# A four-layer kernel on one core: the next layer's Wq, key and value weights folded and split within the closing stage, and both late blocks of the last closing stage loaded ahead of its stores

## The chip, the core and the metric

One core of a Trainium2 chip runs the whole program. The metric is the device time of one execution in microseconds (us); lower is better. The engines are PE (TensorE, matrix products), ACT (ScalarE), DVE (VectorE), POOL (GpSimd) and SP (SyncE), which here only issues DMAs, one after another.

## The reference, cut to what matters

```python
# x: 2 sequences of 1024 rows, 256 wide; cond: 2 x 64
x = x + mixture_of_experts(x, cond)                       # layer 0
for layer in (1, 2, 3):                                   # attention, 16 heads of 64
    xn = layernorm(x) * g_norm                            # g_in in layer 2
    q = xn @ Wq                                           # 256 x 1024
    k, v = split(xn @ Wkv)                                # one key and one value head for all 16
    k, v = concat(cond[0], k), concat(cond[1], v)         # the null key and value
    if layer != 2:
        q = l2norm(q) * q_scale; k = l2norm(k) * k_scale  # logits times 8
        bias = two_layer_network(distance)                # w0, b0, g0, w1, b1, g1, w2, b2
    else:
        q = q / 8; bias = fside                           # an input, 16 x 1024 x 1024
    out = causal_softmax(q @ k.T + bias) @ v
    x = x + layernorm(out @ Wout) * g_out
return x
```

## The kernel before

All matrix products run in a reduced fp32 format, so each operand is split into a high part (a rounding copy) and a low part (value minus high part), and a product is three matmuls (`three_products`, line 216). The rows of `x` stay in SBUF as 16 tiles of 128 rows; four tiles make a block.

Each of the layers 1 to 3 runs four stages. A stage is a `Phase`: each engine has its own list of instructions, linked by semaphores, and a barrier of all engines ends it. So a stage lasts as long as its slowest engine, and nothing of the next stage starts before.

- `prepare_layer` (the preparation). It waits for the layer's inputs (`loaded`). ACT multiplies Wq by the norm's gain (`fold`, line 926) and rounds it (`high_part`, line 932). The null key `k0n` is made (lines 735 to 750), multiplied into Wq (`null_products`, line 701), summed by head (line 771) into 16 further columns of the key and value weights `wx`; DVE scales the other columns by the gain (line 765) and splits `wx` (lines 774 and 776). The first block of `x` is standardised (line 854), turned by PE (line 692) and split (`first_high` on ACT, line 943, and `first_low` on DVE, line 862). DVE writes a mask penalty (line 755) and the null values (six copies, line 760). In layers 1 and 3 the bias network runs too: DVE and ACT alternate over two halves (variances end in line 801, the last silu and low part in lines 814 and 820), PE multiplies, and DVE writes the bias row from PE's last product (line 917). In layer 2 POOL makes the low part of Wq (`low_part`, line 711) and DVE does the products of line 701. In the layers 1 and 3 POOL does those products here and the low part of Wq at the start of `project` (line 1511). In layer 1 DVE also writes four rows of ones (line 870).
- `project`: queries, keys and values of four blocks; SP stores queries and loads first rows of bias.
- `attend`: scores, softmax and outputs; it writes the outputs to `o_dram` and already loads blocks 0 and 1 of them for the next stage.
- `close_layer` (the close). Per tile n of 16: ACT rounds the tile of outputs (`high`, line 1968), DVE makes its low part (`low`, line 2037), both two tiles ahead; PE does 24 matmuls and a product for the null weights; ACT copies the result (line 1974); DVE takes statistics (lines 2042 and 2044). Per block c of 4: variances on DVE (line 2049), root on ACT, and then DVE standardises four tiles (line 2057); for c below 3 POOL multiplies by `gain_out` and adds to `x` (lines 2108 and 2111), and for c = 3 DVE does both (lines 2063 and 2065), after it has waited for POOL's block 2. SP loads block 2 of the outputs once DVE has split block 0, then block 3 once block 1 is split, and then the next layer's inputs. In the last layer SP stores block c - 2 of `x` (`store`, line 1933) behind each of these two loads:

```python
                for c in range(2, NCH):
                    eng.wait_ge(s["o_lo"], CT * (c - 1))
                    load_outputs(eng, t, s[f"in{c % 2}"], c)
                    if out is not None:
                        store(eng, c - 2)
```

The trace names the tiles by where they lie: `bias` is also the space of `wq`, `wx`, `w1` and of the even output blocks, `o_in` that of the odd ones, `v` in the preparation that of the standardised first block.

## Time and profile before

| | |
|---|---|
| median of 3 runs | 2259.14 us (2256.57 to 2260.59) |
| the profiled execution, its own time | 2255.18 us |
| its span in the trace | 2253.4 us |
| mean granted PE clock | 0.943 of full speed |
| close of layer 1 | 855 to 919.7 us of the span |
| preparation of layer 2 | 920.7 to 937.7 |
| close of layer 2 | 1483 to 1547.6 |
| preparation of layer 3 | 1548.6 to 1594.1 |
| close of layer 3, with the last store | 2177.5 to 2253.4 |

A row of a timeline gives the start in us of the span, the duration (of all together where it ends in xN), engine, line, operation, output <- inputs with their shapes, and in brackets the idle time before it and what ended it. Durations of an instruction include the time in which it was issued but held.

### The profile page before, as it was taken

Reading aid. Unit: us, or ns where it says so; the run is one execution under the profiler, and the core shown is the slowest. Engines: PE = TensorE matmul, PEld = TensorE weight load, DVE = VectorE, ACT = ScalarE, POOL = GpSimd, SP = SyncE. Lnnn points to the kernel's source line nnn. Section 1 sums busy time; section 2 is a strip of 40 time slices with the busy share of each in tenths; the row PEclk is TensorE's granted clock in tenths of the full one; section 3 lists DMA queues with packets and bytes.
Section 4 is the critical chain, followed back from the end, with each engine's and each line's share of the span. In section 5 each row is a group of like instructions: output and inputs, shape, how many; then the busy total and the mean of one; then the engine's idle time right before and its main releaser. Section 6 shows DMA issues by size and latency. Waiting matters only on the chain. (4 is left out here: it accounts for less than half of the span.)

```text
span 2253.4 us, 46773 instructions
## 1 busy us (share of the span) xinstructions
PE 1968.3 (87%) x11698; PEld 1427.4 (63%) x11698; DVE 1687.6 (75%) x4098; ACT 1338.7 (59%) x2908; POOL 1077.4 (48%) x1301
## 2 busy tenths in 40 slices
PE   5998595999999998589999999985786999999987
PEld 4887463666666668466666666675554666666667
DVE  4777877877887785658777778758677888887855
ACT  2222565777776674247677667644665777766743
POOL 0443112666766662206666566623124666655622
PEclk8999697999999999799999999997897999999998
DMA  4630167333333343286777888840474333333422
GB/s 119 203 112 26 36 222 257 104 113 112 113 113 113 110 143 110 83 309 189 235 238 239 240 243 242 271 146 15 160 243 159 113 112 112 113 113 113 133 84 102
DMA packets 220535, 338.75 MB, mean 150 GB/s; under 512 B 25766, under 2 KB 102700, under 8 KB 220364
## 3 DMA queue, kind: packets, MB, share of 16 engines
q1 hardware_dynamic: 220364, 336.85, 47.2%
q8 instruction: 60, 0.98, 0.2%
q14 instruction: 111, 0.91, 0.1%
HBM read 250.62 MB, written 102.91 MB: 157 GB/s over the span
## 5 line engine op out<-in xcount | busy, mean ns | idle before, releaser
L1618 POOL TENSOR_SCALAR at_row<-at_row,at_inv 128x129 f32<-128x129 f32 (+7 forms) x384 | 715.5, 1863 | 356.8 <-DVE at_inv L1782 350.4
L1829 ACT ACTIVATE at_row<-at_row,at_nmax 128x129 f32<-128x129 f32 (+7 forms) x768 | 595.3, 775 | 235.2 <-DVE at_nmax L1801 233.7
L1801 DVE CUSTOM_DVE_ANT_0 at_row<-at_s,bias,at_row 128x128 f32<-128x128 f32 (+7 forms) x768 | 617.4, 810 | 70.6 <-PE at_s L1729 36.3
L1741 PE MATMUL at_t<-ident,at_row 128*128 128x128 f32 x3456 | 545.6, 281 | 40.1 <-ACT at_pt L1822 34.1
L1741 PEld LDWEIGHTS at_t<-ident,at_row 128*128 128x128 f32 x3456 | 393.2, 142 | 244.6 <-issue 164.5
L1728 PE MATMUL at_s<-k_hh,q_hl 128*128 128x512 f32 (+3 forms) x1152 | 463.1, 402 | 45.8 <-SPq L1686 21.6
L1757 PE MATMUL at_o<-at_pt,v 128*64 128x512 f32 (+3 forms) x2304 | 437.2, 501 | 5.6 <-ACT at_pt L1822 2.5
L1633 DVE COPY at_pt<-at_t 128x128 f32<-128x128 f32 (+3 forms) x576 | 277.9, 483 | 177.8 <-PE at_t L1741 174.1
L1729 PE MATMUL at_s<-k_lp,q_h 65*128 65x512 f32 (+3 forms) x1152 | 394.4, 354 | 0.0
L1822 ACT ACTIVATE at_pt<-at_t 128x512 f32<-128x512 f32 (+2 forms) x576 | 306.8, 533 | 133.9 <-PE at_t L1741 128.7
L1728 PEld LDWEIGHTS at_s<-k_hh,q_hl 128*128 128x128 f32 x1152 | 225.4, 196 | 79.3 <-DVE at_nmax L1801 31.5
L1757 PEld LDWEIGHTS at_o<-at_pt,v 128*64 128x64 f32 x2304 | 143.3, 136 | 179.2 <-issue 142.1
L1618 DVE TENSOR_SCALAR at_row<-at_row,at_inv 128x129 f32<-128x129 f32 (+7 forms) x384 | 253.0, 659 | 2.1 <-issue 0.9
L1729 PEld LDWEIGHTS at_s<-k_lp,q_h 65*128 65x128 f32 x1152 | 225.7, 196 | 17.7
L1829 ACT ACTIVATION_READ_ACCUMULATOR at_row<-at_row,at_nmax 128x1 f32 x768 | 144.0, 187 | 0.0
L1884 POOL COPY null_w<-at_row 128x2 f32 (+1 forms) x384 | 71.2, 186 | 132.8 <-DVE at_row L1618 70.4
L216 PE MATMUL cl_y<-wo_h,cl_oh 128*128 128x256 f32 x384 | 117.5, 306 | 15.5 <-DVE cl_ol L2037 15.5
L1872 POOL COPY at_row<-neg_null 128x2 f32 (+1 forms) x384 | 71.9, 188 | 104.2 <-PEq L145 80.5
L521 POOL TENSOR_TENSOR moe_hid_l<-moe_hid,moe_hid_h 128x512 fp32r<-128x512 f32 x40 | 51.7, 1293 | 142.2 <-ACT moe_hid_h L506 142.1
L216 PE MATMUL cl_y<-wo_l,cl_oh 128*128 128x256 f32 x384 | 112.0, 292 | 0.0
L216 PE MATMUL cl_y<-wo_h,cl_ol 128*128 128x256 f32 x384 | 111.8, 291 | 0.0
L1517 POOL TENSOR_TENSOR o_in<-pj_qn,o_in 128x512 fp32r<-128x512 f32 x26 | 36.1, 1392 | 123.2 <-ACT o_in L1275 123.2
(249 smaller groups left out, 2855.9 us busy)
## 6 DMA issues: line engine op xcount, KB each, us to landing
q_hl<-q_dram SPq DMA_DIRECT2D x192, 256.0 KB, 4.3
q_dram<-o_in SPq DMA_DIRECT2D x76, 512.0 KB, 3.7
bias<-bands_dram SPq DMA_DIRECT2D x64, 512.0 KB, 5.4
q_h<-q_dram SPq DMA_DIRECT2D x96, 256.0 KB, 5.0
o_dram<-o_sb SPq DMA_DIRECT2D x96, 256.0 KB, 4.6
bands_dram<-brow_dram SPq DMA_DIRECT2D x2, 8192.0 KB, 32.2
bias<-corners_dram SPq DMA_DIRECT2D x256, 64.0 KB, 4.3
bias<-in_fside SPq DMA_DIRECT2D x32, 448.0 KB, 4.8
```

The lines of the kernel that those rows point to most:

```text
L216: last = eng.matmul(out, left[a], right[b], start=start and n == 0, stop=stop and n == len(pairs) - 1)
L1618: return eng.tensor_scalar(cells, cells, inv[:, i:i + 1], None, ALU.mult)
L1633: copy(bass.AP(one.tensor, one.offset, [one.ap[0], [pitch, blocks], [1, P]]), t_ps[m % NTR][:, 0:blocks * P].rearrange("p (c i) -> p c i", ...
L1728: eng.matmul(out, q_hl[:, g % 2, side, at], t["k_hh"][:, b, c:c + n], start=True, stop=False)
L1729: last = eng.matmul(out, q_h1[0:DH + 1, g % 2, side, at], t["k_lp"][0:DH + 1, b, c:c + n], start=False, stop=True)
L1741: last = eng.transpose(t_ps[m % NTR][:, c * P:(c + 1) * P], row[:, u % RING, here:here + P], t["ident"][:])
L1757: last = eng.matmul(o_ps[side * DH:(side + 1) * DH, i0:BANK], t["v"][:, turn.half_of(GU * g) * NT + j, :], pt[g % 2][:, side, at + i0:at + ...
L1801: eng.tensor_tensor_reduce(out=row[:, u % RING, ZERO:ZERO + width], in0=s_ps[u % 2][:, 0:width], in1=bt[:, lo:lo + width], scale=-1.0, sca ...
L1822: return eng.activation(out, in_, ACT.Copy)
L1829: eng.activation(cells, cells, ACT.Exp, scale=-1.0, bias=nmax[:, i:i + 1], accum_out=rsum[:, i:i + 1]).then_inc(s["exp"], 1)
L1872: eng.tensor_copy(null_cell(u, 2), nulls(turn, "neg_null", u)).then_inc(s["null_in"], 1)
L1884: eng.tensor_copy(nulls(turn, "null_w", u), null_cell(u, 2)).then_inc(s["null_out"], 1)
```

## The change

The work on Wq and `wx` is cut into functions. For layer 1 they still run in the preparation. For the layers 2 and 3 (`coming`) they run in the close of the layer before: ACT folds and rounds Wq in tiles 11 to 14; DVE squares (or, for layer 2, scales) the null key and scales `wx` at tile 11, ends the null key of layer 3 at tile 13, sums the products at tiles 14 and 15, and splits `wx` before the last tile's statistics; POOL clears the spare columns of `wx` and does both products between its work on block 1 and block 2, and for layer 2 makes the low part of Wq after block 2. In layer 3's inputs the bias network's are loaded last. The rows of ones of layer 1 go from DVE to POOL. In the last close SP issues both loads first and all four stores behind them. To make room for `wq_h`, `wq_l`, `wx_h` and `wx_l` in the close, three tiles of the projection share space with tiles of the attention.

```diff
+WEIGHT_STEPS = ["norm_in", "norm", "folded", "k0n", "prod", "hi", "lo", "wx_zero"]
...
+def fold_gain(eng, t, s, k):
+    i = t["inputs"]
+    eng.activation(i["wq"][:, k, :], i["wq"][:, k, :], ACT.Copy, scale=i["gain"][:, k:k + 1]).then_inc(s["folded"], 1)
+def high_weights(eng, t, s, k):
+    eng.wait_ge(s["folded"], k + 1)
+    eng.activation(t["wq_h"][:, k, :], t["inputs"]["wq"][:, k, :], ACT.Copy).then_inc(s["hi"], 1)
+def low_weights_of(eng, t, s):
+    eng.wait_ge(s["hi"], KD)
+    for k in range(KD):
+        for n in range(2):
+            at = slice(n * BANK, (n + 1) * BANK)
+            eng.tensor_tensor(t["wq_l"][:, k, at], t["inputs"]["wq"][:, k, at], f32(t["wq_h"][:, k, at]), ALU.subtract
+                              ).then_inc(s["lo"], 1)
...
+def null_root(eng, s, space):
+    eng.wait_ge(s["norm_in"], 1)
+    eng.activation(space["ss"][:], space["ss"][:], ACT.Sqrt).then_inc(s["norm"], 1)
...
+def null_key(eng, own, t, s, space):
+    i, ss, k0n = t["inputs"], space["ss"], space["k0n"]
+    own.step(eng.scalar_tensor_tensor(t["kscale"][:], t["kscale"][:], 8.0, i["qcol"][:], ALU.mult, ALU.mult))
+    own.step(eng.scalar_tensor_tensor(i["kscale"][:], i["kscale"][:], 8.0, i["qs"][:], ALU.mult, ALU.mult))
+    eng.wait_ge(s["norm"], 1)
+    own.step(eng.tensor_scalar(ss[:], ss[:], 1e-12, None, ALU.max))
+    own.settle()
+    own.step(eng.reciprocal(ss[:], ss[:]))
+    own.settle()
+    eng.scalar_tensor_tensor(k0n[:], i["k0"][:], ss[:, 0:1], i["kscale"][:], ALU.mult, ALU.mult).then_inc(s["k0n"], 1)
...
+def null_products(eng, t, s, space):
+    eng.wait_ge(s["k0n"], 1)
+    for k in range(KD):
+        eng.wait_ge(s["folded"], k + 1)
+        eng.tensor_tensor(space["prod"][:, k, :].rearrange("p (h d) -> p h d", h=H),
+                          t["inputs"]["wq"][:, k, :].rearrange("p (h d) -> p h d", h=H),
+                          space["k0n"][:].unsqueeze(1).to_broadcast([P, H, DH]), ALU.mult).then_inc(s["prod"], 1)
...
+def key_gains(eng, own, t):
+    wx, gain = t["inputs"]["wx"], t["inputs"]["gain"]
+    for k in range(KD):
+        own.step(eng.tensor_scalar(wx[:, k, 0:NUL], wx[:, k, 0:NUL], gain[:, k:k + 1], None, ALU.mult))
+def null_sums(eng, own, t, s, space, k):
+    eng.wait_ge(s["prod"], k + 1)
+    own.step(eng.tensor_reduce(t["inputs"]["wx"][:, k, NUL:NUL + H], space["prod"][:, k, :].rearrange("p (h d) -> p h d", h=H),
+                               AX.X, ALU.add))
+def split_key_weights(eng, own, t, s):
+    wx = t["inputs"]["wx"]
+    eng.wait_ge(s["wx_zero"], 1)
+    own.settle()
+    own.step(eng.tensor_copy(t["wx_h"][:], wx))
+    own.settle()
+    own.step(eng.tensor_tensor(t["wx_l"][:], wx, f32(t["wx_h"][:]), ALU.subtract))
...
-                    null_products(eng)
-                    eng.wait_ge(s["prod"], 1)
-                else:
-                    low_part(eng)
-                    eng.wait_ge(s["lo"], 1)
+                if layer == 1:
+                    eng.memset(i["wx"][:, :, NUL + H:], 0.0).then_inc(s["wx_zero"], 1)
+                    eng.wait_ge(s["cleared"], 2)
+                    eng.wait_ge(s["wx_zero"], 1)
+                    for n in range(4):
+                        eng.memset(f32(t["q_h1"][DH:DH + 1, n // 2, n % 2, :]), 1.0).then_inc(s["ones"], 1)
+                        eng.wait_ge(s["ones"], n + 1)
+                    null_products(eng, t, s, space)
+                    eng.wait_ge(s["prod"], KD)
...
                 loaded(eng)
                 if not normed:
-                    null_square()
                     first_rows()
                     first_standardize()
-                    null_products(eng)
                     null_values()
                     first_low()
-                    null_columns()
-                    xo.settle()
+                    eng.wait_ge(s["v0_in"], 1)
+                    eng.wait_ge(s["x_lo"], KD)
                     return
-                null_square()
+                if layer == 1:
+                    null_square(eng, own, t, s, space, True)
...
-                null_key()
+                if layer == 1:
+                    null_key(eng, own, t, s, space)
...
                 for m in range(2):
                     silu(2 + m)
                     low_silu(2 + m)
-                    if m == 0:
-                        ones()
-                null_columns()
+                if layer == 1:
+                    for k in range(KD):
+                        null_sums(eng, own, t, s, space, k)
+                    split_key_weights(eng, own, t, s)
...
-        xb = sb("pj_xb", [P, CT, D])
+        xb = t["o_sb"][:].rearrange("p n i -> p (n i)").rearrange("p (n i) -> p n i", n=CT)
...
-            qn = sb("pj_qn", [P, NQN, BANK])
+            qn = t["wo_raw"].rearrange("p a n -> p (a n)").rearrange("p (n i) -> p n i", n=NQN)
...
+    WEIGHTS_AT = 11
+    coming = None if inputs is None else inputs[-1]
...
                 for c in range(2, NCH):
                     eng.wait_ge(s["o_lo"], CT * (c - 1))
                     load_outputs(eng, t, s[f"in{c % 2}"], c)
-                    if out is not None:
-                        store(eng, c - 2)
                 if inputs is not None:
                     load_inputs(eng, t, *inputs)
                 for n in range(2):
                     eng.wait_ge(s[f"in{n}"], 16)
                 if out is not None:
-                    for c in range(NCH - 2, NCH):
+                    for c in range(NCH):
                         store(eng, c)
                     eng.wait_ge(s["stored"], 16 * NCH)
...
+                    if coming and WEIGHTS_AT <= n < WEIGHTS_AT + 2 * KD:
+                        if n == WEIGHTS_AT:
+                            inputs_loaded(eng, t)
+                        if n < WEIGHTS_AT + KD:
+                            fold_gain(eng, t, s, n - WEIGHTS_AT)
+                        else:
+                            high_weights(eng, t, s, n - WEIGHTS_AT - KD)
+                    if coming == 3 and n == WEIGHTS_AT + 1:
+                        null_root(eng, s, space)
...
+                    if coming and n == WEIGHTS_AT:
+                        inputs_loaded(eng, t)
+                        null_square(eng, own, t, s, space, coming != 2)
+                        key_gains(eng, own, t)
+                    if coming == 3 and n == WEIGHTS_AT + 2:
+                        null_key(eng, own, t, s, space)
+                    if coming and n >= NTT - KD:
+                        null_sums(eng, own, t, s, space, n - NTT + KD)
+                if coming:
+                    split_key_weights(eng, own, t, s)
                 statistics(NTT - 1)
                 variances(NCH - 1)
                 close(NCH - 1)
...
                     eng.tensor_tensor(t["x"][:, at, :], t["x"][:, at, :], half, ALU.add).then_inc(s["added"], 1)
+                    if coming and c == NCH - 3:
+                        inputs_loaded(eng, t)
+                        eng.memset(t["inputs"]["wx"][:, :, NUL + H:], 0.0).then_inc(s["wx_zero"], 1)
+                        null_products(eng, t, s, space)
+                if coming == 2:
+                    low_weights_of(eng, t, s)
+                    eng.wait_ge(s["lo"], 2 * KD)
+                elif coming:
+                    eng.wait_ge(s["prod"], KD)
...
+        for layer in (0, 1, 2, 3):
+            w = inputs_of(layer)[0] if layer else None
             with tensors(nc) as (sbl, _):
                 for part in "hl":
                     t[f"wo_{part}"] = sbl(f"wo_{part}", [P, NPAIR, D], FR)
+                    t[f"xt_{'high' if part == 'h' else 'low'}"] = t[f"wo_{part}"][:].rearrange("p a n -> p (a n)").rearrange(
+                        "p (c k i) -> p c k i", c=2, k=KD)
                 t["o_sb"] = sbl("o_sb", [P, 2, BANK])
                 t["wo_raw"] = sbl("wo_raw", [P, NPAIR, D])[:]
-                attend(nc, t, w, bias)
-                close_layer(nc, t, out if layer == 3 else None, inputs_of(layer + 1) if layer < 3 else None)
+                if layer:
+                    t["gain_out"] = t["gains_out"][layer % 2]
+                    attend(nc, t, w, None if layer != 2 else a["fside"])
+                if layer == 3:
+                    close_layer(nc, t, out, None)
+                    break
+                with tensors(nc) as (sbq, _):
+                    for part in "hl":
+                        t[f"wq_{part}"] = sbq(f"wq_{part}", [P, KD, H * DH], FR)
+                        t[f"wx_{part}"] = sbq(f"wx_{part}", [P, KD, 2 * P], FR)
+                    if layer:
+                        close_layer(nc, t, None, inputs_of(layer + 1))
+                    normed = layer + 1 != 2
+                    if normed:
+                        t["bands_n"] += 16
+                    with tensors(nc) as (sbp, _):
+                        t["brow_sb"] = sbp("brow_sb", [H, BROW])
+                        prepare_layer(nc, t, layer + 1)
+                        project(nc, t, normed, None if normed else a["fside"])
```

## Rows read from the trace of the kernel before

**Rows 1.** The page's first part: busy us of each engine, share of the span, instructions.

```profile
PE 1968.3 (87%) x11698; PEld 1427.4 (63%) x11698; DVE 1687.6 (75%) x4098; ACT 1338.7 (59%) x2908; POOL 1077.4 (48%) x1301
```

**Rows 2.** The chain that ended last, two steps in the last close: start, us.

```profile
2214.99 0.39 SPq L1933
2215.43 8.90 DMA o_in<-o_dram
```

**Rows 3.** ACT's timeline, last close: start, us, operation, [idle before, releaser].

```profile
2224.35 1.06 ACT L1968 ACTIVATE cl_oh<-o_in 128x1024 fp32r<-128x1024 f32 x1 [6.78 <-DMA o_in<-o_dram]
```

**Rows 4.** DVE's timeline, preparation of layer 2.

```profile
924.64 2.35 DVE L701 TENSOR_TENSOR lw_prod<-bias,lw_k0n 128x1024 f32<-128x1024 f32 x2
...
928.58 3.82 DVE L760 COPY v0m<-in_v 64x8 f32<-64x8 f32 x6
...
934.22 2.33 DVE L771 TENSOR_REDUCE bias<-lw_prod 128x16 f32<-128x1024 f32 x2
...
937.05 0.69 DVE L776 TENSOR_TENSOR wx_l<-bias,wx_h 128x512 fp32r<-128x512 f32 x1
```

**Rows 5.** DVE's splits of output blocks, all closes: shortest, median, longest ns.

```profile
L2037 DVE TENSOR_TENSOR cl_ol<-bias,cl_oh x24: 1217/1222/2883, 856.9 to 2216.7; 128x1024 fp32r<-128x1024 f32 x24
```

**Rows 6.** POOL's split of Wq in layer 2's preparation: shortest, median, longest ns.

```profile
L711 POOL TENSOR_TENSOR wq_l<-bias,wq_h x4: 1257/1482/3139, 925.0 to 931.0; 128x512 fp32r<-128x512 f32 x4
```

**Rows 7.** DVE's timeline, preparation of layer 1.

```profile
245.71 1.22 DVE L787 TENSOR_TENSOR bias<-rb_mm,bias 128x1024 f32<-128x1024 f32 x1 [0.35 <-PE rb_mm L216]
...
261.33 2.11 DVE L870 MEMSET q_h<- 1x512 f32 x4 [0.16 <-issue]
```

**Rows 8.** ACT's timeline, preparation of layer 2.

```profile
926.78 1.08 ACT L943 ACTIVATE xt_high<-lw_xtr 128x512 fp32r<-128x512 f32 x2 [1.89 <-PE lw_xtr L692]
```

**Rows 9.** POOL's timeline, close of layer 1.

```profile
900.35 3.27 POOL L2111 TENSOR_TENSOR x<-x,cl_y 128x1024 f32<-128x1024 f32 x1
...
911.51 2.39 POOL L2111 TENSOR_TENSOR x<-x,cl_y 128x1024 f32<-128x1024 f32 x1
```

**Rows 10.** DVE's timeline, close of layer 1.

```profile
898.47 2.88 DVE L2037 TENSOR_TENSOR cl_ol<-o_in,cl_oh 128x1024 fp32r<-128x1024 f32 x1
...
914.43 0.43 DVE L2042 BATCH_NORM_STATS2 cl_stats<-cl_y 128x6 f32<-128x256 f32 x1 [0.75 <-ACT cl_y L1974]
...
918.44 1.23 DVE L2065 TENSOR_TENSOR x<-x,cl_y 128x1024 f32<-128x1024 f32 x1
```

**Rows 11.** DVE's timeline, preparation of layer 3.

```profile
1548.67 0.23 DVE L737 TENSOR_TENSOR lw_k0n<-in_k 128x64 f32<-128x64 f32 x1 [1.06 <-PEq L83]
...
1570.03 0.15 DVE L743 SCALAR_TENSOR_TENSOR kscale<-kscale,in_qcol 128x1 f32<-128x1 f32 x1
...
1570.62 0.28 DVE L750 SCALAR_TENSOR_TENSOR lw_k0n<-in_k,lw_ss,in_kscale 128x64 f32<-128x64 f32 x1
...
1573.92 1.88 DVE L801 TENSOR_SCALAR rb_rstd<-rb_mv 128x4 f32<-128x4 f32 x1
...
1580.34 0.64 DVE L760 COPY v0m<-in_v 64x8 f32<-64x8 f32 x6
...
1592.83 1.27 DVE L917 TENSOR_SCALAR brow_sb<-rb_mm,in_b 16x1024 f32<-16x1024 f32 x1
```

**Rows 12.** POOL's timeline, preparation of layer 3.

```profile
1571.08 4.70 POOL L701 TENSOR_TENSOR lw_prod<-bias,lw_k0n 128x1024 f32<-128x1024 f32 x2 [20.61 <-DVE lw_k0n L750]
```

**Rows 13.** PE's timeline, last product in the preparation of layer 3.

```profile
1591.70 0.63 PE L216 MATMUL rb_mm<-rb_uh,rb_w2l 128*128 128x512 f32 x1
```

**Rows 14.** DVE's timeline, close of layer 2.

```profile
1535.52 1.38 DVE L2057 TENSOR_SCALAR cl_y<-cl_y,cl_mv,cl_rstd 128x256 f32<-128x256 f32 x4
...
1546.38 1.22 DVE L2065 TENSOR_TENSOR x<-x,cl_y 128x1024 f32<-128x1024 f32 x1
```

**Rows 15.** Two stretches of layer 2's projection: busy us, then clock, DMA.

```profile
938.00:950.00 12.00, 10.91 (x40) 8.77 (x41) 4.83 (x16) 3.24 (x7) 0.00 (x0) 0.75 0.62 179
...
965.00:980.00 15.00, 14.32 (x69) 11.16 (x68) 9.98 (x25) 6.85 (x14) 0.00 (x0) 1.00 0.83 276
```

143 lines of the change are left out of this document (43 added, 100 removed).

## The prediction, made before the changed kernel ran

> **What bounds the kernel now.** I read the page's first part first: PE is busy for 87% of the span [rows 1]. That is an average; this change touches only stage ends, where PE rests. So I read next the chain that ended last. It ends in the last close, and there a load of outputs waits its turn: SP stands in front of a store that needs POOL's block 0, issues the store at 2214.99, then the load, whose 2 MB take 8.90 us [rows 2]. ACT idles 6.78 us for it [rows 3], PE behind ACT.
>
> The third view is DVE's timeline between the stages. The preparation of layer 2 ends when DVE ends, at 937.05 + 0.69 = 937.74, and nearly all it does after 924.7 is weight work [rows 4].
>
> The fourth view decides the price of moved work: how DVE and POOL get on together. A split of 1024 columns costs DVE 1.22 us, but up to 2.88 us [rows 5]; the long ones stand beside POOL's additions. At 898.47 DVE issued one [rows 10] while POOL worked; it ended at 901.35, and POOL's addition, issued at 900.35, took 3.27 instead of 2.39 [rows 9]. So the two take turns, whole instructions at a time. The six copies of null values took 3.82 us beside POOL [rows 4] and 0.64 alone [rows 11]; the variance of line 801 took 1.88 us beside POOL's product [rows 11, 12] and ended with it. The Trainium skill, page "SBUF — State Buffer", section "Who interferes with whom", calls this port pair an exclusive lock, taken by DVE's two-input operations, copies, casts and tensor_scalar; the trace agrees in the rows just named.
>
> **Part by part.** Stage ends decide, so I work out the new end of each touched stage.
>
> *Preparation of layer 1.* The four rows of ones leave DVE: 2.11 us [rows 7]. ACT, PE and the bias row stand behind them. On POOL they run near 226 us, where it is idle. Gain 2.1 us; at least 1, if their writes hold DVE's early steps, and 2.1 at most.
>
> *Preparation of layer 2.* What is left ends with the split of x: ACT's high part ends at 926.78 + 1.08 = 927.86 [rows 8], DVE's second low part, 0.7 us, at 928.5. Penalty and copies, free of POOL, end before that. 937.74 - 928.5 = 9.2 us gained. The cover of this number is the penalty's DMA into `k_lp`, which is issued some 3 us earlier too.
>
> *Close of layer 1, taking layer 2's weights.* POOL's block 1 ends at 900.35 + 3.27 = 903.6 [rows 9]. The scaled null key waits for that end, and the two gains follow; POOL's first product (2.35 us each: 4.70 for two [rows 12]) runs 904.3 to 906.7. DVE's low part of tile 14 gets the turn until 907.8, the second product until 910.2; DVE's variances of block 2 wait for it, ACT's root for them, and on ACT are queued the high parts of Wq and PE's copies. PE's last tile starts 1 to 2 us late, which the tail hides. Block 2 is standardised at 913.5, POOL's two operations (2.39 each) end at 918.3. DVE's sums, 2.33 us for both [rows 4], end at 917.1; its cast waits until 918.3; then DVE and POOL's four pieces of the low part, 1.26 us each alone [rows 6], take turns: the split of `wx` ends at 920.5. From the last statistics to the end DVE took 914.43 to 918.44 + 1.23 = 919.67, or 5.24 us [rows 10]; with three more turns lost to POOL (0.8, 0.7 and 1.1 us left of a piece) it is 7.8. New end 928.3, 8.6 us later. Lowest, with no turns at all: sums and split stand 1.6 us in front of the last statistics, so 1.6. Highest: 11 (below). I take 8.6, since the rows show turns wherever both engines work.
>
> *Preparation of layer 3.* The square at its head goes, 0.23 us [rows 11], and its sum, which I put at as much: 0.5 us. The null key (1570.03 to 1570.90) goes too; I count nothing for it, since in the same place of layer 1 DVE still waits 0.35 us for PE's product [rows 7]; 0.9 is the upper bound. The variance's wait for POOL goes, 1.88 less the 0.15 of the other small operations, 1.7 us [rows 11]. At the end the sums and splits go, but the bias row waits for PE's last product, 1591.70 + 0.63 = 1592.33 [rows 13], against its start at 1592.83: 0.5 us. Their whole length was covered by PE, and this cover stays. Gain 2.7 us.
>
> *Close of layer 2, taking layer 3's.* Here is a new wait. POOL stands before its first product until DVE has the null key, and this comes behind the standardised block 2: 1535.52 + 1.38 = 1536.9 [rows 14], held 1.2 us by squares and gains at tile 11, then 0.9 us for the key itself: 1539.0. POOL's products take until 1543.8, and only then come its two operations on block 2, which began at 1537 before. DVE meanwhile stands before each sum, and ends the second at 1545.0. Its cast waits for POOL's multiplication (1546.3), its subtraction for POOL's addition (1549.0), and is done at 1549.65; the last statistics and all behind it, 5.24 us, end at 1554.9, against 1546.38 + 1.22 = 1547.6 [rows 14]. Cost 7.3 us. Lowest, without turns, 3.8 (the sum at 1545.0, split 1.2, tail 5.24); highest 9.8.
>
> *Last close.* The load of block 3 is issued when block 1 is split, not behind a store, as in the two other closes, where ACT does not wait. Gain 6.8 us [rows 3]. The final store is alone at the end as before. SP's stores 0 to 2, now later, have nobody behind them.
>
> *Moves that cost nothing:* ACT's 4 us of folding and rounding lie in its rests between tiles (it is busy 59% of the span [rows 1], and if PE kept it busy there, each us would push PE's last tile); the inputs have landed by tile 11; the aliased tiles are dead when reused; SP issues the same DMAs.
>
> **Sum:** -2.1 - 9.2 + 8.6 - 2.7 + 7.3 - 6.8 = -4.9 us. Against the profiled execution's 2255.2 us that is 2250.3; the median of the runs stands 4 us above this execution, so I forecast 2259.1 - 4.9 = **2254.2 us**. A measurement of this kernel can tell about 0.2%, or 4.5 us, from no change.
>
> **The rivals.**
>
> *B, few turns.* If DVE and POOL pass each other more often than I assume, both closes cost less. With none, 1.6 and 3.8: the sum is -15.4. The rows exclude that; halfway gives -10.2 and 2249. For it: POOL's wait at 924.97 let two of DVE's products through, since it got its first piece only after 3.14 us [rows 4, 6].
>
> *C, every DVE operation takes turns,* the sums also. Each of the two sums then waits for one more POOL operation, 2.4 us per close in all: 11.0 and 9.8, the sum is 0.0, 2259. Nothing in the rows shows a sum beside POOL. The same section of the Trainium skill says that a reduction never contends on this chip; by it C falls away and the sum stays -4.9. No row here shows it.
>
> *D, the late load only changes its place.* ACT would wait elsewhere in the last close, and 6.8 us are not gained: +1.9, 2261. Against it: the two other closes load in this order.
>
> *E, slower: PE's clock.* The longer tails leave PE idle longer in front of each projection. Layer 2's begins at three quarters of full speed on the mean, between 1.2 and 2.4 GHz, and has the full 2.4 GHz at 965 [rows 15]. At 1.2 GHz PE does half the work. If the clock stayed low for 12 us more in each of the projections of layers 2 and 3, with PE the bound in them, each would lose 6 us: +7.1, 2266. It decides from 9.4 us lost in all. Against: the idle stretch before layer 2's projection is no longer than before (the close grows as much as the preparation shrinks), that before layer 3's 5 us longer.
>
> **How the numbers follow.** Forecast 0.46, within 2.5 us either way; the bound 2254.6 parts it 0.27 faster, 0.19 the same. B 0.21, faster. C 0.19, the same. D 0.05, the same. E 0.09, slower. So faster 0.48, same 0.43, slower 0.09. The range is 2246 to 2260: it holds the forecast, B down to -13 and C, and leaves out D, E and B's far end.
>
> **What would show it.** The preparation of layer 2 lasting 7.8 us (17.0 before), that of layer 3 42.8 (45.5), the close of layer 2 longer by 7 us with POOL idle before line 701's product and its addition of block 2 ending near 1549, and ACT without a wait for `o_in` in the last close. Wrong would be a close of layer 1 that grows by under 5 or over 11 us, a sum of over 1.3 us beside POOL (then C), or a wait of ACT for the inputs at tile 11.

## The result, and the profile after

The changed kernel takes 2247.34 us (median of 5 runs, 2245.59 to 2250.14) against 2259.14 us beside it: ratio 0.9947, 95% interval 0.9933 to 0.9962. It is faster, by 11.8 us in the medians and by 9.6 us in the profiled executions (2255.18 and 2245.59 us). The forecast was 4.9 us; the range held the time, near its lower end. Measured again later, the same kernel gained 9.0 us in the medians (ratio 0.9961).

I cut both traces at the ends of the stages and compare stretch by stretch. A close runs from ACT's first instruction of it to DVE's last, a preparation from there to DVE's end (layer 2) or the end of the bias row (layers 1 and 3).

```
us                        before   after   measured   forecast
preparation, layer 1       47.69   45.33     -2.4       -2.1
close of layer 1           64.15   71.64     +7.5       +8.6
preparation, layer 2       18.07    9.03     -9.0       -9.2
close of layer 2           64.23   69.95     +5.7       +7.3
preparation, layer 3       46.50   44.09     -2.4       -2.7
last close                 72.00   64.22     -7.8       -6.8
sum                                          -8.4       -4.9
projection and attention, three stretches    -1.3        0
```

The page's first part shows next to nothing of this; PE's share goes from 87% [rows 1] to 88%:

```profile
span 2243.8 us, 46782 instructions
PE 1965.3 (88%) x11698; PEld 1421.4 (63%) x11698; DVE 1693.1 (75%) x4092; ACT 1338.8 (60%) x2911; POOL 1085.5 (48%) x1307
```

**The close of layer 1.** DVE's timeline after the change, from the variances of block 2 on (start, us, engine, line, what; in brackets the idle time in front). The rows of before are [rows 10].

```profile
906.57 1.69 DVE L2095 TENSOR_SCALAR cl_rstd<-cl_mv 128x4 f32<-128x4 f32 x1
...
911.89 1.19 DVE L705 TENSOR_REDUCE bias<-lw_prod 128x16 f32<-128x1024 f32 x1
...
914.85 1.75 DVE L714 CAST wx_h<-bias 128x512 fp32r<-128x512 f32 x1
916.63 1.63 DVE L716 TENSOR_TENSOR wx_l<-bias,wx_h 128x512 fp32r<-128x512 f32 x1
918.30 0.43 DVE L2088 BATCH_NORM_STATS2 cl_stats<-cl_y 128x6 f32<-128x256 f32 x1
...
919.90 2.78 DVE L2103 TENSOR_SCALAR cl_y<-cl_y,cl_mv,cl_rstd 128x256 f32<-128x256 f32 x4
...
923.97 1.23 DVE L2111 TENSOR_TENSOR x<-x,cl_y 128x1024 f32<-128x1024 f32 x1
```

POOL in the same stretch (before: [rows 9]):

```profile
902.36 5.87 POOL L690 TENSOR_TENSOR lw_prod<-bias,lw_k0n 128x1024 f32<-128x1024 f32 x2
911.50 2.40 POOL L2164 TENSOR_TENSOR cl_y<-cl_y,gain_out 128x1024 f32<-128x1024 f32 x1 [3.27 <-DVE cl_y L2103]
913.98 2.34 POOL L2167 TENSOR_TENSOR x<-x,cl_y 128x1024 f32<-128x1024 f32 x1
916.27 5.61 POOL L651 TENSOR_TENSOR wq_l<-bias,wq_h 128x512 fp32r<-128x512 f32 x4
```

Read the two side by side. The variances, 0.17 us of work, take 1.69 us, since a product of POOL is running. The cast and the subtraction of `wx` (0.43 and 0.69 us alone) take 1.75 and 1.63; the last standardising takes 2.78 instead of 1.38. But the sum at 911.89 takes its 1.19 us though POOL's multiplication runs beside it all the time: a sum takes no turn. Behind the variances stands ACT's root, and behind that, in ACT's order, PE's copies:

```profile
908.30 0.20 ACT L1995 ACTIVATE cl_rstd<-cl_rstd 128x4 f32<-128x4 f32 x1 [3.23 <-DVE cl_rstd L2095]
```

**The close of layer 2.** DVE's timeline, then POOL's (before: [rows 14]):

```profile
1533.89 0.28 DVE L682 SCALAR_TENSOR_TENSOR lw_k0n<-in_k,lw_ss,in_kscale 128x64 f32<-128x64 f32 x1
...
1536.68 1.22 DVE L705 TENSOR_REDUCE bias<-lw_prod 128x16 f32<-128x1024 f32 x1 [1.95 <-POOL lw_prod L690]
...
1539.00 1.22 DVE L705 TENSOR_REDUCE bias<-lw_prod 128x16 f32<-128x1024 f32 x1 [0.55 <-POOL lw_prod L690]
1540.33 1.23 DVE L714 CAST wx_h<-bias 128x512 fp32r<-128x512 f32 x1
1541.59 2.71 DVE L716 TENSOR_TENSOR wx_l<-bias,wx_h 128x512 fp32r<-128x512 f32 x1
...
1548.34 1.23 DVE L2111 TENSOR_TENSOR x<-x,cl_y 128x1024 f32<-128x1024 f32 x1
```

```profile
1534.26 4.70 POOL L690 TENSOR_TENSOR lw_prod<-bias,lw_k0n 128x1024 f32<-128x1024 f32 x2 [6.60 <-DVE lw_k0n L682]
1538.93 2.33 POOL L2164 TENSOR_TENSOR cl_y<-cl_y,gain_out 128x1024 f32<-128x1024 f32 x1
1541.35 2.40 POOL L2167 TENSOR_TENSOR x<-x,cl_y 128x1024 f32<-128x1024 f32 x1
```

POOL idles 6.60 us for the null key and DVE in front of both sums, as the prediction had it; the cast waits for the multiplication, the subtraction for the addition.

**The preparations and the last close.** The six copies of null values take 0.64 us instead of 3.82 [rows 4], and the preparation of layer 2 ends with the split of `x`. In that of layer 3 DVE idles 2.71 us in front of the bias row, for PE [rows 11, 13]. In the last close ACT's split of tile 12 has no idle time in front of it any more [rows 3]; SP stands at its stores with nobody behind it. DVE, DVE, ACT, SP:

```profile
930.77 0.64 DVE L823 COPY v0m<-in_v 64x8 f32<-64x8 f32 x6
932.94 1.29 DVE L911 TENSOR_TENSOR wo_l<-lw_xtr,wo_h 128x512 fp32r<-128x512 f32 x2 [1.54 <-ACT wo_h L977]
...
1592.39 1.27 DVE L962 TENSOR_SCALAR brow_sb<-rb_mm,in_b 16x1024 f32<-16x1024 f32 x1 [2.71 <-PE rb_mm L218]
```

```profile
2214.64 1.06 ACT L2005 ACTIVATE cl_oh<-o_in 128x1024 fp32r<-128x1024 f32 x1
```

```profile
2212.24 28.09 SPq L1972 DMA_DIRECT2D out<-x  x4
```

**PE's clock** (busy time by engine, granted clock, DMA share, GB/s; the two stretches of [rows 15], counted from the end of the preparation):

```profile
934.20:946.20 12.00, 10.56 (x40) 8.54 (x41) 4.71 (x17) 3.24 (x7) 0.00 (x0) 0.76 0.58 164
961.20:976.20 15.00, 14.53 (x69) 11.38 (x68) 10.00 (x25) 6.96 (x14) 0.00 (x0) 1.00 0.85 289
```

The projection starts between the two levels, 1.2 and 2.4 GHz, as before (0.76 for 0.75), and is at the upper one (1.00) 27 us later, as before. The first 12 us of layer 3's projection have 0.86 in both kernels. The longer tails cost the projections nothing. At the start of the closes the clock did make a difference; see the experiments.

### The profile page after: what moved, and what is told of

It reads as the page before. It is cut to its first block and busy times, and to the rows that moved or that the text cites. A ratio compares the mean times of both kernels' runs of the same rounds, so it can differ in the third digit from the quotient of the medians.

```text
span 2243.8 us, 46782 instructions
## 1 busy us (share of the span) xinstructions
PE 1965.3 (88%) x11698; PEld 1421.4 (63%) x11698; DVE 1693.1 (75%) x4092; ACT 1338.8 (60%) x2911; POOL 1085.5 (48%) x1307
## 5 line engine op out<-in xcount | busy, mean ns | idle before, releaser
L1552 POOL TENSOR_TENSOR o_in<-wo_raw,o_in 128x512 fp32r<-128x512 f32 x26 | 36.1, 1394 | 123.5 <-ACT o_in L1310 123.5
```

## The experiments

Twelve kernels, each timed in five rounds beside the kernel before. The stretches of all of them, in us; "sum" is that of the five stage ends without the first preparation, which all kernels but the one with only the last close changed share:

```
                          close 1  prep 2  close 2  prep 3  last    sum   ratio to before (95%)
before                      64.15   18.07    64.23   46.50  72.00  264.95
changed                     71.64    9.03    69.95   44.09  64.22  258.93  0.9947 (0.9933-0.9962)
changed, again              71.49    9.04    70.20   44.31  63.95  258.99  0.9961 (0.9946-0.9976)
stores back                 71.74    9.04    70.14   44.23  70.34  265.49  0.9982 (0.9968-0.9997)
last close only             64.24   18.09    64.64   46.48  65.18  258.63  0.9969 (0.9953-0.9986)
low part in prep. 2         68.18   11.24    70.82   44.83  63.98  259.05  0.9974 (0.9959-0.9990)
key one tile earlier        71.48    9.04    69.12   44.67  63.96  258.27  0.9961 (0.9945-0.9976)
inputs first                72.04    9.04    70.46   44.54  64.25  260.33  0.9963 (0.9943-0.9983)
inputs first, spread        68.79    9.03    68.23   43.33  64.27  253.65  0.9937 (0.9914-0.9960)
no work on POOL             65.76    9.04    65.82   44.69  64.06  249.37  0.9923 (0.9908-0.9938)
sums in preparations        69.67   11.11    68.19   44.98  64.74  258.69  0.9950 (0.9932-0.9968)
sums, low part in prep.     66.35   13.31    68.25   44.96  65.11  257.98  0.9927 (0.9908-0.9945)
the same, key moved         65.84   15.37    66.90   45.15  65.21  258.47  0.9938 (0.9922-0.9955)
key moved, no late start    65.12   13.31    66.84   45.11  65.20  255.58  0.9940 (0.9925-0.9955)
```

A stage repeats within 0.3 us in the close of layer 1 (71.48 to 71.74 in four kernels that share it), but not everywhere: that of layer 2 takes 69.95 to 70.82 us in the same instructions, and the last close 63.95 to 65.21. The long stretches between, with the same instructions in all kernels, vary more: 584.0 to 590.4, 545.2 to 551.4, 579.4 to 584.0 us. So I read an edit's effect from its stages, and the ratios only as a check.

**PE's clock at the start of a close.** Nearly all that the closes vary by is this. PE has rested when a close begins (5.04 us before its first product in the last one), and its first products of 256 columns run at 1.2 GHz and take 0.41 us each; then the clock rises to 2.4 GHz and they take 0.28. ACT waits meanwhile for the null rows (`cl_vps`), and all tiles follow behind. The stretch from 6.5 to 12.5 us of the last close, in the kernel before, the changed one, and the one with only the last close changed (busy time by engine, granted clock, DMA share, GB/s):

```profile
2184.00:2190.00 6.00, 6.00 (x30) 5.08 (x30) 0.00 (x0) 0.29 (x2) 0.00 (x0) 0.80 0.00 0
2182.20:2188.20 6.00, 6.00 (x37) 5.03 (x36) 0.42 (x1) 1.34 (x3) 0.00 (x0) 0.99 0.00 0
2187.10:2193.10 6.00, 6.00 (x30) 5.09 (x30) 0.00 (x0) 0.32 (x2) 0.00 (x0) 0.80 0.00 0
```

A granted clock of 0.99 says that in the changed kernel the rise came about when this stretch began, some 6.6 us into the close; at 0.80 it came some 2.3 us later, at 8.9 us. The table gives, for each close, when ACT starts on the null rows (us from its start), and the close's length with the difference from the kernel before taken off, so as it would be at that kernel's clock:

```
                          null rows at            length at before's clock
                          c. 1   c. 2   last      close 1  close 2  last
before                   11.10  11.19  12.17        64.15    64.24  72.00
changed                  11.68  11.05  11.15        71.05    70.09  65.24
changed, again           11.56  11.30  10.91        71.03    70.09  65.22
stores back              11.80  11.21  11.31        71.04    70.12  71.20
last close only          11.21  11.58  12.14        64.14    64.24  65.21
low part in prep. 2      10.85  11.91  10.91        68.42    70.09  65.23
key one tile earlier     11.53  11.04  10.91        71.05    69.27  65.22
inputs first             11.66  11.57  11.19        71.49    70.08  65.23
inputs first, spread     11.28  11.32  10.91        68.60    68.09  65.53
no work on POOL          11.49  11.11  11.01        65.37    65.90  65.21
sums in preparations     10.90  11.91  11.71        69.87    67.47  65.21
sums, low part in prep.  10.87  11.92  12.07        66.58    67.52  65.21
the same, key moved      11.40  11.48  12.16        65.53    66.61  65.23
key moved, no late start 10.72  11.43  12.16        65.50    66.59  65.21
```

On the right, closes with the same instructions agree within 0.05 us. What makes the clock rise early or late in an execution is open: closes with the same instructions show both.

**The two halves of the change.** Stores back:

```
                 for c in range(2, NCH):
                     load_outputs(eng, t, s[f"in{c % 2}"], c)
+                    if out is not None:
+                        store(eng, c - 2)
...
-                    for c in range(NCH):
+                    for c in range(NCH - 2, NCH):
```

> The changed kernel with one part undone: in the last close SP again issues each store between two loads, as before the change. Theory (late load): the last close grows back from 64.2 to about 72 us and ACT stands again some 6.8 us in front of tile 12 for a load of outputs; everything in front of it stays as in the changed kernel; the profiled execution is 6.8 to 7.8 us longer than the changed kernel's 2245.6, near 2253, and the weights' part alone is worth 2 to 3 us against the kernel before. Rival (the load was hidden, the gain of the last close comes from elsewhere, for instance from PE's clock): the last close stays near 65 us, the time near 2246 to 2248.

The last close grows back by 6.1 us (6.0 at the same clock), and ACT stands where it stood before:

```profile
2224.92 1.06 ACT L2007 ACTIVATE cl_oh<-o_in 128x1024 fp32r<-128x1024 f32 x1 [6.60 <-DMA o_in<-o_dram]
```

The profiled execution takes 2255.18 us, as long as that of the kernel before, and not the 2253 expected: its first long stretch took 590.0 us. The other half alone, the kernel before with this edit:

```
-                    if out is not None:
-                        store(eng, c - 2)
...
-                    for c in range(NCH - 2, NCH):
+                    for c in range(NCH):
```

> The kernel before with only the last close's order changed (both loads in front of the stores), the weights prepared as before. Theory: all stages up to the last close keep their lengths, the last close falls from 72.0 to 64 to 65 us: 6.8 to 7.8 us gained, near 2248 in a profiled execution. If the two parts of the change add up, this gain and that of the weights alone (the run with stores put back) sum to the 9.6 us of the whole. Rival (the parts interact, the last close gains only once the weight work has moved): a gain under 4 us.

It gains 6.8 us in the last close and nothing elsewhere (the 0.4 us more in the close of layer 2 are the clock's); the ratio gives 7.0 us (0.31% of 2261), that of the stores put back 4.1 us, with an interval from 0.7 to 7.2. The halves add up to 11.1 us by the ratios; the whole gave 11.8 and, again, 8.8, so the ratios neither show nor exclude that the halves act on each other. By the stages the weight work brings far less than its preparations show: -2.4 + 7.5 - 9.0 + 5.7 - 2.4 = -0.6 us, or -1.1 at the same clock.

**The changed kernel again.**

> The changed kernel itself once more, beside the runs of this call. Theory: closes of 71.6, 70.0 and 64.2 us and preparations as before; a median some 0.5% under that of the kernel before. The long stretches of projection and attention between the stages, whose instructions are the same in all kernels, lie within 3 us of 585, 547 and 582 us; what they vary by here is no effect of an edit.

All stages repeat within 0.3 us (the closes within 0.02 at the same clock); the ratio is 0.9961, 3 us from the first 0.9947 and inside the width of both intervals. The 0.5% expected of the median was 0.4%. The stretches between lie at 587.8, 548.1 and 582.6 us.

**POOL's share of what the closes lose.** The products and the low part are left out, their tiles filled with zeros at the start of the close:

```
+                if coming:
+                    eng.memset(space["prod"][:], 0.0).then_inc(s["prod"], KD)
+                if coming == 2:
+                    eng.memset(f32(t["wq_l"][:]), 0.0).then_inc(s["lo"], 1)
...
-                        null_products(eng, t, s, space)
+                        eng.wait_ge(s["k0n"], 1)
```

> The changed kernel without POOL's weight work in the closes: the products of Wq with the null key (layers 2 and 3) and the low part of layer 2's Wq are left out and their tiles filled with zeros at the start of the close, where POOL is idle; DVE and ACT do all their weight work in its place. Theory (POOL's operations cost the closes through DVE: each is a turn at the common port, and block 2 comes late): the sums no longer wait, the slip of PE's tile 13 in the close of layer 1 goes (1.9 us), the tail behind the last statistics is 5.24 us in both; closes of 66 to 67 us against 71.6 and 70.0. What is left over the 64.2 of before is DVE's own work, of which the second sum and the split of wx (2.5 to 3 us) stand behind PE's last tile. Rival (DVE's own moved work is nearly the whole cost): closes of 69 us or more.

65.76 and 65.82 us, just under the 66 to 67 expected; the slip of tile 13 is gone, and the tail is 5.23 us in both. So of the 7.5 and 5.7 us that the closes lose, POOL's work makes 5.9 and 4.1, and DVE's own work 1.6 on each. At the same clock the split is 5.7 and 1.2 of 6.9, and 4.2 and 1.7 of 5.9. (POOL still waits for the null key here, and its block 2 comes late for it: that part of its cost in the close of layer 2 is not taken away.) This is the cleanest reading of the study. DVE does all its gains, sums and splits here, and the second sum and the split stand just in front of the last statistics:

```profile
1537.22 1.19 DVE L700 TENSOR_REDUCE bias<-lw_prod 128x16 f32<-128x1024 f32 x1
1538.52 0.88 DVE L709 CAST wx_h<-bias 128x512 fp32r<-128x512 f32 x1
1539.43 0.69 DVE L711 TENSOR_TENSOR wx_l<-bias,wx_h 128x512 fp32r<-128x512 f32 x1
```

**POOL's low part moved into the preparation of layer 2.**

```
                 if coming == 2:
-                    low_weights_of(eng, t, s)
-                    eng.wait_ge(s["lo"], 2 * KD)
```

and the same four subtractions behind POOL's `memset` in the preparation.

> The changed kernel, but POOL's four pieces of the low part of layer 2's Wq are moved from the end of the close of layer 1 into the preparation of layer 2, still on POOL. Theory (DVE and POOL take turns at their common port): in the close of layer 1 the stretch from the last statistics to DVE's end goes back from 6.9 us to 5.24, and the cast and the subtraction of wx are no longer stretched, so the close is 1.7 to 2.2 us shorter (71.6 to about 69.6); in the preparation DVE's standardising and copies now meet POOL's pieces, which gives back 1 to 2 us. In all 0 to -1 us. Rival (the longer tail comes from the waits at tiles 14 and 15, not from POOL): the tail stays at 6.9 us. Rival (few turns): the preparation doesn't grow, so the whole gains 1.7 us or more.

The close loses 3.3 to 3.5 us of its length, 1.66 of it in the tail (5.24 us again), 0.94 in the subtraction of `wx` (0.69 for 1.63). The rest, 0.8 us, lies in front of the first tile and is the clock's, so the edit gives 2.6 us, more than the 1.7 to 2.2 expected. Both rivals fall, and with the preparation's 2.2 us the whole is within the 0 to -1 us forecast. The preparation pays its 2.2 us, all in one place: its four standardising operations take 3.57 us instead of 1.38, beside POOL's 5.03.

```profile
928.89 3.57 DVE L910 TENSOR_SCALAR v<-x,lw_x_mv,lw_x_rstd 128x256 f32<-128x256 f32 x4
```

```profile
926.97 5.03 POOL L805 TENSOR_TENSOR wq_l<-bias,wq_h 128x512 fp32r<-128x512 f32 x4
```

**The null key a tile earlier in the close of layer 2.**

```
-                    if coming == 3 and n == WEIGHTS_AT + 2:
+                    if coming == 3 and n == WEIGHTS_AT + 1:
```

> The changed kernel, but in the close of layer 2 DVE makes layer 3's null key at tile 12 instead of tile 13. POOL stands 6.6 us in front of its first product for that key. Theory (DVE's own backlog in front of the last statistics sets the end of the close, part of it made of turns with POOL): POOL starts its products some 3 us earlier, but they now take turns with the standardising of block 2 and the last split, and the close of layer 2 gets shorter by 0.5 to 1.5 us (69.95 to about 69). Rival (POOL's wait for the key is the whole cost of this close): it gets shorter by about 3 us. All other stages unchanged.

0.8 to 1.1 us, not 3: POOL's wait for the key falls from 6.60 to 3.43 us, but its products then meet the standardising of block 2, whose four operations take 4.82 us.

**All weight work earlier: the inputs loaded first.**

```
-    WEIGHTS_AT = 11
+    WEIGHTS_AT = 5
...
+                if inputs is not None:
+                    load_inputs(eng, t, *inputs)
                 for c in range(2, NCH):
...
-                    if coming and c == NCH - 3:
+                    if coming == 2 and c == 1:
+                        low_weights_of(eng, t, s)
+                    if coming and c == 0:
```

with both sums and the split at tile 14.

> The changed kernel with the weight work placed earlier in the closes of layers 1 and 2: the inputs are loaded before the blocks of outputs, gains and folding begin at tile 5, POOL's products follow block 0 and its low part (layer 2) block 1, and both sums and the split of wx stand on DVE at tile 14. Nothing else differs. Theory (what the closes lost, 7.5 and 5.7 us, is the wait of DVE for products, POOL's late block 2 and the turns behind it): POOL idles for 8 to 9 us between blocks, so its products cost nothing, sums (2.4) and split (1.8) come before the last statistics with some 2 us of them covered; each close costs 0.5 to 3 us against before instead of 7.5 and 5.7, and the tail behind the last statistics is 5.24 us in both. 7 to 11 us less than the changed kernel: 2235 to 2239 in a profiled execution. Rival (it is the amount of the moved work on DVE and ACT that sets the closes, wherever it stands): the closes keep 70 us or more, less than 3 us gained. Rival (the inputs' load in front delays the outputs' loads): ACT waits for block 0 or 1 of the outputs at the start of the close, some us lost there.

A plain miss: 72.0 and 70.5 us; by the letter the first rival's. The second falls: ACT never waits for a load of outputs. POOL's idle time between blocks was 5.1 and 5.4 us in the kernel before, not the 8 to 9 of the expectation, and POOL's products, 4.7 us together undisturbed, had to go in there. DVE did not idle then, and each split that meets POOL's work is held (1.22 us alone); so are the variances, ACT behind them for 3.23 us, and PE behind ACT:

```profile
889.44 2.89 DVE L2083 TENSOR_TENSOR cl_ol<-bias,cl_oh 128x1024 fp32r<-128x1024 f32 x1
...
911.90 3.58 DVE L2103 TENSOR_SCALAR cl_y<-cl_y,cl_mv,cl_rstd 128x256 f32<-128x256 f32 x4
```

PE's lost time shows best in ACT's copies of PE's product, tile by tile, in us from the start of the close of layer 1 (3.1 us a tile undisturbed):

```
tile                       3     4     5     6     7     8     9    12    13    14    15
before                  23.0  26.1  29.2  32.3  35.4  38.5  41.6  50.9  54.0  57.1  58.5
changed                 23.5  26.6  29.6  32.7  35.8  38.8  41.9  51.1  56.0  58.4  59.8
inputs first            23.4  26.5  30.4  32.9  36.0  39.3  44.1  52.9  55.9  59.0  60.4
key moved, all in prep. 23.2  26.3  29.4  32.4  35.5  38.6  41.6  50.9  53.9  57.0  58.4
```

The changed kernel starts 0.6 us late by the clock and slips once, by 1.8 us at tile 13 (ACT's wait of 3.23 us), of which it makes 0.6 up at the next tile; with the inputs first the slip of 1.8 us comes at tile 9 instead, behind one of 0.9 at tile 5.

**The same, spread.** ACT and DVE split three tiles ahead, the sums stand at tiles 10 and 11, the split of `wx` at 12.

```
-    AHEAD, SLOTS = 2, 4
+    AHEAD, SLOTS = 3, 4
...
-                    if coming and n == NTT - 2:
-                        for k in range(KD):
-                            null_sums(eng, own, t, s, space, k)
+                    if coming and NTT - 6 <= n < NTT - 6 + KD:
+                        null_sums(eng, own, t, s, space, n - NTT + 6)
+                    if coming and n == NTT - 4:
                         split_key_weights(eng, own, t, s)
```

> The kernel with the inputs loaded first and the weight work from tile 5 on, with two more edits: ACT and DVE split three tiles ahead of PE instead of two, and the sums stand at tiles 10 and 11, the split of wx at tile 12, instead of all at tile 14. Theory (what a close pays is DVE's work that is late when PE's last tile ends, plus the tiles that PE waits for a split held by POOL): the copy of the last tile's product comes at 58.5 to 59.5 us from the start of the close, as in the kernel before, and the end 5.6 to 6.5 us behind it: 64 to 66 us per close against 71.6 and 70.0, 9 to 13 us in all. Rival (the common port of DVE and POOL has no room left in a close, wherever the work stands): PE's tiles slip again in the middle, closes of 68 us or more.

68.8 and 68.2 us, by the letter the rival's. PE still slips at tile 9 (in the close of layer 2 at tile 12 too), since ACT's wait for the variances (3.46 us here) does not depend on how far the splits run ahead. But it has the shortest sum of stages of all kernels that do the whole work, 5.3 us under the changed one (4.9 at the same clock).

**Sums and split in the preparations.** The products are kept in the idle `wo_raw` and summed there:

```
-                    if coming and n >= NTT - KD:
-                        null_sums(eng, own, t, s, space, n - NTT + KD)
-                if coming:
-                    split_key_weights(eng, own, t, s)
...
                     null_values()
+                    for k in range(KD):
+                        null_sums(eng, own, t, s, space, k)
+                    split_key_weights(eng, own, t, s)
                     first_low()
```

> The changed kernel, but the two sums and the split of wx on DVE stand in the preparations of layers 2 and 3 (in layer 3's at the place they had before the change) instead of in the closes; POOL's products, gains, key, folding and POOL's low part stay in the closes. Theory (DVE's work between the last tiles and the last statistics is what the closes pay; in the preparation of layer 3 the same work stands beside waits of 3.0 and 2.7 us and is free): the close of layer 2 falls from 69.95 to 65 to 66 us, that of layer 1 from 71.6 to 67 to 68, the preparation of layer 2 grows by 2 to 2.5 us, that of layer 3 by 0 to 0.5: 6 to 7 us gained in all. Rival (the closes pay for POOL's late block 2, not for DVE's backlog): closes of 69 us or more, and the whole is slower than the changed kernel.

Half right. The preparation of layer 2 cost the 2 to 2.5 us expected (2.1), that of layer 3 0.9 for at most 0.5, and the closes fell by only 2.0 and 1.8 (1.2 and 2.6 at the same clock). With POOL's low part in the preparation too (the edit of the run above, on top of this one):

> As the kernel with sums and split in the preparations, and POOL's low part of layer 2's Wq too is moved into the preparation of layer 2. In the run that moved this part alone the close of layer 1 fell by 3.5 us and the preparation grew by 2.2. Theory (turns at the common port cost DVE time where it is on the path): the close of layer 1 comes to 65 to 66 us; in the preparation POOL's four pieces now meet the standardising, the null values and the split of wx, which grows by 4 to 6 us against the changed kernel's 9.0; against the kernel with sums and split in the preparations the whole is within 1.5 us of equal. Rival (the pieces find free time in the preparation while DVE sums): 2 us or more gained against it.

the close of layer 1 came to 66.35 us (65 to 66 expected) and the preparation grew by 4.3, as expected; the sum of the stages is 0.7 us under the kernel before this one, so its rival falls. The close of layer 2 stayed at 68.25. Its timeline names the second cause, which the rival of the run above had: once DVE is on time, POOL's block 2, late for the key and the products, falls on the last standardising. DVE, then POOL:

```profile
1546.57 5.00 DVE L2114 TENSOR_SCALAR cl_y<-cl_y,cl_mv,cl_rstd 128x256 f32<-128x256 f32 x4
```

```profile
1546.02 2.33 POOL L2171 TENSOR_TENSOR cl_y<-cl_y,gain_out 128x1024 f32<-128x1024 f32 x1
1548.43 2.34 POOL L2174 TENSOR_TENSOR x<-x,cl_y 128x1024 f32<-128x1024 f32 x1
```

So in this close the two costs stand beside each other rather than in a row: with the sums and the split away it is still 3.3 us longer than before at the same clock, and the standardising alone is held by 3.6 (5.00 for 1.38). In the close of layer 1 the two moves do not hide each other: at the same clock the low part moved alone gave 2.6 us, sums and split alone 1.2, both together 4.5.

**The key moved by a tile in both closes, and POOL's low part held back until `x` is standardised.**

```
-                        null_square(eng, own, t, s, space, coming != 2)
+                        if coming == 3:
+                            null_square(eng, own, t, s, space, True)
...
+                    if coming == 2 and n == WEIGHTS_AT + 1:
+                        null_square(eng, own, t, s, space, False)
-                    if coming == 3 and n == WEIGHTS_AT + 2:
+                    if coming == 3 and n == WEIGHTS_AT + 1:
                         null_key(eng, own, t, s, space)
...
                 if layer == 2:
+                    eng.wait_ge(s["x_norm"], 1)
                     for k in range(KD):
```

> As the kernel with sums, split and low part all in the preparations, with two more moves: DVE makes the null key one tile later in the close of layer 1 (behind the variances of block 2, for which ACT and behind it PE wait) and one tile earlier in the close of layer 2 (so that POOL's products no longer push block 2 into the last standardising, which took 5.0 us instead of 1.38 there); and POOL's low part in the preparation of layer 2 waits until x is standardised. Theory (turns cost only where DVE's next step is on the path): the slip of PE's tile 13 in the close of layer 1 (1.9 us) goes, closes of 64.5 to 65.5 us against 66.4 and 68.3, the preparation of layer 2 12 us against 13.3: 5 to 6 us gained over that kernel, about 9 over the changed kernel. Rival (the turns only move to other operations of DVE on the path): under 2 us gained in the three stages together.

The slip of tile 13 is gone (table above), and the closes fell by 0.5 and 1.4 us (1.1 and 0.9 at the same clock), but the preparation grew by 2.1 where it should have shrunk by 1.3. So the 5 to 6 us expected did not come, and the result is the rival's: the turns only moved. The wait put POOL's four pieces beside six copies of 0.1 us each, and four of the six were held for a whole piece:

```profile
926.46 4.91 DVE L833 COPY v0m<-in_v 64x8 f32<-64x8 f32 x6
```

```profile
926.02 5.32 POOL L808 TENSOR_TENSOR wq_l<-bias,wq_h 128x512 fp32r<-128x512 f32 x4 [3.33 <-DVE v L913]
```

With that wait for `x_norm` taken out again, and nothing else changed:

> The kernel with the null key moved by a tile in both closes and all else in the preparations, with one edit taken back: POOL's low part in the preparation of layer 2 no longer waits until x is standardised, since that put its four pieces beside DVE's six small copies of null values (4.91 us instead of 0.64). Theory (each DVE operation, however small, lets one POOL operation in front of it): the copies fall back to 0.64 us, the standardising of four operations is stretched to 3.6 in their place, the preparation of layer 2 lasts 13.3 us again against 15.4, the closes stay at 65.8 and 66.9: about 2 us gained over that kernel, 4 to 5 over the changed one. Rival (the length of the preparation was chance): 15 us again.

13.31 us, as expected, and the closes at the same clock stay as they were (65.50 and 66.59 us for 65.53 and 66.61); the copies take 0.64 us again:

```profile
927.14 0.64 DVE L832 COPY v0m<-in_v 64x8 f32<-64x8 f32 x6
```

Its stages are 3.4 us shorter than the changed kernel's (3.8 at the same clock; 4 to 5 were expected). The ratios of this kernel (0.9940), of the one with sums and low part in the preparations (0.9927) and of the spread one (0.9937) all lie under both of the changed kernel's, but the intervals overlap: that they beat it is shown by the stages (3.8, 1.9 and 4.9 us at the same clock), not by the times.

## Why the prediction was right, and what was off

**Right, by its own steps.** The preparation of layer 2 lasts 7.9 us from its first row against the 7.8 forecast; that of layer 3 42.9 against 42.8. ACT's wait in the last close is gone, [rows 3], and the halves' runs show 6.0 and 6.8 us for it at the same clock; 6.8 was forecast. In the close of layer 1 the split of `wx` ends at 918.26, which is 920.2 in before's time (the close starts 1.96 us sooner); the forecast was 920.5. In the close of layer 2 the tail behind the last statistics is the 5.24 us of before to 0.01 us.

**Off.** The forecast moved 3.6 us less than the stages did, in three terms.

- *"with three more turns lost to POOL ... it is 7.8"*: 6.9 us. POOL's pieces end at 921.9, before DVE's last two operations; only the variances and the standardising lost turns. With the split 0.3 us sooner, this makes the 1.1 us. (This close began 0.6 us late by the clock. At the same clock it costs 6.9 us, 1.7 less than forecast.)
- *"held 1.2 us by squares and gains at tile 11"*: the null key came at 1534.2, 1537.9 in before's time, instead of 1539.0, and the subtraction of `wx` ended at 1548.0 for 1549.65. The squares are indeed held (1.89 us), but in before the split of tile 14 was held there by the same addition of POOL; the hold is the same one and was counted on top. This is 1.1 of the 1.6 us; the rest is that POOL's two operations on block 2 took 4.8 us together (1538.93 to 1543.75), not the 5.2 from 1543.8 to 1549.0, and the subtraction behind them 0.1 less.
- *The last close, 6.8*: 7.8 in this pair of executions, but the step is right. ACT's wait for PE's null rows at the start is 9.86 us before and 8.85 after: PE's clock rose some 2.3 us sooner in this execution (0.99 against 0.80 in the stretch shown above), and the products that ran at the lower level meanwhile in the other make the 1.0 us. The kernel with only this edit has 0.80 too and a wait of 9.83, and gains 6.8. The forecast had no term for the clock at the start of a close.

The preparation of layer 1 gained 2.4 us, 0.3 over what was called the most; the idle time in front of the rows of ones (0.16 us) went with them, and the first products took 0.1 us less. The rest, to 9.6 us, is 1.3 us in the stretches between, and their spread is larger than that.

**What was luck.** The forecast had the weight work alone cost 1.9 us and the whole gain come from the last close; by the stages it gained 0.6 to 1.1 us. The direction of the whole was safe by the last close. That the medians' 2247.34 us lies in the range at all is narrow: the two missed sizes, the clock and the long stretches all fell on the fast side. The gain came out near the 10.2 us of rival B, but not for B's reason, except for the 0.9 us of turns that were not lost in the first close's tail.

**The rivals.** C (sums take turns too) falls: the sum takes 1.19 us beside POOL's multiplication of 2.40. This is the rule of the Trainium skill, page "SBUF — State Buffer", section "Who interferes with whom", that a reduction never contends, which no row of before had shown; the trace now agrees, in both closes. B (few turns) falls: wherever both worked, the turns were there, up to one of POOL's operations for each of DVE's. D falls with the run with the stores put back. E falls: the granted clock in layer 2's projection is 0.76 and then 1.00 (0.75 and 1.00 before), in the first 12 us of layer 3's 0.86 in both, and the stretches of projection and attention behind them are no longer than before (545.4 for 545.6 us, 582.0 for 583.4).

**Not settled.** The first stretch of projection and attention took 584.6 and 584.0 us in the two kernels without the weight edit, and 584.9 to 590.4 (mean 587.8) in the twelve with it. The difference builds up in steps far into attention, where the granted clock dips (0.96 to 0.98 in some stretches of 100 us, 1.00 in others). Two against twelve is no proof; were it an effect of the change, the 2.4 us of layer 1's preparation would be given back there. No run was made for it. Nor for this: in the closes of layers 1 and 2 PE's undisturbed pace is 3.07 us a tile in all kernels with the weight edit and 3.10 in the two without it (3.10 in every last close), which gives back some 0.4 us a close.

## What to carry to other kernels

Work moved onto "idle" engines of the closing stage wasn't free, since two engines share one thing: price a POOL operation by what DVE does beside it: up to one whole POOL operation for each DVE operation, however small. Put POOL's work beside DVE's sums and statistics, not beside chains of small copies or scalings, and keep it away from an operation for which another engine's queue stands still (here the variances, ACT's root, PE's copies). And look first at the order of a queue: the two lines that put loads in front of stores brought 6 to 7 us, several times what all the weight work brought after its costs (about 1 us by the stages; 4.1 us by the ratio, with 0.7 to 7.2 as its interval). When two profiles of one stage are compared, first see where PE's clock rose in each: here that alone moved a close by up to 1.3 us.

## What the runs showed of the hardware that was not expected

- What DVE loses beside POOL goes by the number of operations that meet and by the length of POOL's, not by the size of DVE's: six copies of 0.64 us in all took 4.91 us beside four POOL operations of some 1.3 us (four copies were held for 1.2 us each, two passed); four scalings of 1.38 us in all took 3.57 beside the same four, and 4.82 to 5.00 beside two of 2.3 us; one split of 1.22 us took 2.89.
- Sums (1.19 us) and batch-norm statistics (0.42 us) keep their length beside POOL in every kernel here.
- POOL's four rows of ones in layer 1's preparation (2.24 us from 225.32) did not lengthen what DVE did beside them: four products of 1.67 us together, the same as without, of which only the last ran beside the rows, and the statistics behind.
- At the start of a close, in the same instructions, PE's clock rose from 1.2 to 2.4 GHz at about 6.6 us in one execution and 8.9 us in another, and the whole close moved by 1.0 us.
